# Second layer of a graph network: two weight slots swap roles each block, output weights split in the last head, three output tiles between the last weighted values

## The reference, cut to what matters

```python
cond = silu(emb @ f_w1 + f_b1) @ f_w2 + f_b2
for i in range(4):
    y = cond_layer_norm(x, cond, s1_w[i], s1_b[i], b1_w[i], b1_b[i])
    y = sparse_attention(y, src, dst, wq[i], bq[i], wk[i], bk[i], wv[i], bv[i], wo[i], bo[i])   # 4 heads of 128
    x = x + y
    y = cond_layer_norm(x, cond, s2_w[i], s2_b[i], b2_w[i], b2_b[i])
    x = x + relu(y @ m_w1[i] + m_b1[i]) @ m_w2[i] + m_b2[i]
```

## Time and profile before

| | us |
|---|---|
| runs, median of 3 (lowest, highest) | 2396.46 (2392.19, 2398.84) |
| the profiled execution, its own time | 2400.95 |
| span of its profile | 2399.2 |
| TensorE busy | 2106.9 (88%) |
| VectorE, ScalarE, GpSimd busy | 1584.8, 961.6, 643.8 |
| TensorE clock granted, mean | 0.948 of full speed |

### The profile page before, as it was taken

One profiled execution on the slowest core, in us unless ns is written; L12 is line 12 of the kernel. 1 busy time (PEld: TensorE's weight loads), 2 busy tenths in 40 slices (PEclk: granted clock), 3 DMA queues, 4 the chain that ended last, 5 costly groups with the idle time before them and its releaser, 6 DMA issues. The chain is left out here.

```text
span 2399.2 us, 38632 instructions
## 1 busy us (share of the span) xinstructions
PE 2106.9 (88%) x14446; PEld 1593.5 (66%) x14446; DVE 1584.8 (66%) x3086; ACT 961.6 (40%) x1418; POOL 643.8 (27%) x472
## 2 busy tenths in 40 slices
PE   6888979999899998899999899999898997878783
PEld 5885537788787887787788687788684544333331
DVE  8995344778564778554778554778655046898974
ACT  1112213666333666333666333666330031243442
POOL 0000015200543200544200544200420000476773
PEclk9999989999999999999999999999999997898997
DMA  1012301789511788511788611688946000000001
GB/s 59 34 45 46 104 23 61 130 149 159 118 57 37 136 141 151 128 41 52 117 146 155 138 38 56 114 148 147 201 103 145 16 20 2 0 0 0 1 1 43
DMA packets 488314, 195.74 MB, mean 82 GB/s; under 512 B 441241, under 2 KB 457625, under 8 KB 488133
## 3 DMA queue, kind: packets, MB, share of 16 engines
q1 hardware_dynamic: 488133, 193.31, 39.2%
HBM read 62.94 MB, written 25.45 MB: 37 GB/s over the span
## 5 line engine op out<-in xcount | busy, mean ns | idle before, releaser
L670 PE MATMUL psum<-turned_probability_parts,values_high 125*128 125x125 bf16 x1600 | 283.1, 223 | 55.0 <-DMA turned_probability_parts<-probability_parts 33.8
L859 DVE CUSTOM_DVE_ANT_0 probabilities<-psum,counts 125x1250 f32<-125x1250 f32 x160 | 233.6, 1460 | 125.7 <-PE psum L672 125.2
L1383 ACT ACTIVATE probabilities<-probabilities,row_peaks 125x1250 f32<-125x1250 f32 x160 | 214.5, 1341 | 177.4 <-DVE row_peaks L863 177.3
L672 PE MATMUL psum<-turned_probability_parts,values_low 125*128 125x125 bf16 x1600 | 282.4, 222 | 0.0
L671 PE MATMUL psum<-turned_probability_parts,values_high 125*128 125x125 bf16 x1600 | 282.2, 222 | 0.0
L1575 DVE SCALAR_TENSOR_TENSOR probability_parts<-probabilities,row_masses,probability_parts 125x1250 bf16<-125x1250 f32 x160 | 245.2, 1533 | 11.4 <-ACT probability_parts L1393 9.0
L1902 POOL TENSOR_TENSOR logs_and_shifts<-logs_by_source,target_shifts_spread 125x1250 f32<-125x1250 f32 x80 | 208.0, 2617 | 126.5 <-ACT target_shifts_spread L2035 67.0
L1393 ACT ACTIVATE probability_parts<-probabilities,row_masses 125x1250 bf16<-125x1250 f32 x160 | 214.0, 1338 | 41.8 <-DVE row_masses L871 34.3
L2141 PE MATMUL psum<-probabilities_turned,values_and_ones 125*65 125x512 f32 (+1 forms) x480 | 200.1, 563 | 22.1 <-ACT probabilities_turned L2052 11.8
L670 PEld LDWEIGHTS psum<-turned_probability_parts,values_high 125*128 125x128 bf16 x1600 | 159.6, 100 | 76.5 <-issue 73.5
L453 ACT ACTIVATE norm_std<-norm_moments,norm_eps 125x1 f32<-125x1 f32 x120 | 35.2, 294 | 345.6 <-DVE norm_moments L449 345.6
(11 more groups left out here) (291 smaller groups left out, 5048.4 us busy)
## 6 DMA issues: line engine op xcount, KB each, us to landing
weight_stage<-in_L_gnn_m_w SPq DMA_DIRECT2D x32, 256.0 KB, 2.7
block_inputs_kept<-nodes SPq DMA_DIRECT2D x8, 896.0 KB
counts_kept<-counts_by_target_rows SPq DMA_DIRECT2D x10, 625.0 KB, 3.6
logs_kept<-counts SPq DMA_DIRECT2D x1, 5468.8 KB
nodes<-block_inputs_kept SPq DMA_DIRECT2D x12, 448.0 KB
turned_probability_parts<-probability_parts SPq DMA_TRANSPOSE x320, 3.6
counts_by_target<-counts_kept SPq DMA_DIRECT2D x2, 2187.5 KB
logs_by_source<-logs_kept SPq DMA_DIRECT2D x1, 4375.0 KB
```

Source lines behind the costliest of these rows:

```text
L670: pe.matmul(out, lh, rh, start=first, stop=False, skip_group_check=True)
L672: return pe.matmul(out, ll, rh, start=False, stop=last, skip_group_check=True)
L859: dve.tensor_tensor_reduce(prob[0:TILE, T % 2, :], scores, fx.count_src[0:TILE, i, 0:NODES], scale, MASKED, ALU.add, ALU.max, p[:, 0:1]).t ...
L1383: nc.scalar.activation(prob[0:TILE, T % 2, :], prob[0:TILE, T % 2, :], ACT.Exp, bias=fx.peak[0:TILE, T % 2, 1:2], accum_out=fx.mass[0:TILE ...
```

## The change

The two slots are allocated with the same three layouts each. `scored_slot(b) = (b + 1) % 2` holds queries, keys and later m1; `attended_slot(b) = b % 2` holds wv, the attended rows and the first keys of the odd heads, later wo and then m2. So wo goes where the attended rows were (free once their low parts are made, at tile 3 of the last head; the fourth piece and the bias row wait for the last scores, as keys lie there), and m1 goes where queries and keys were. Slot A grows from 20000 to 20096 bytes, and everything above it moves up by 96.

- **Loads.** Pieces 14 and 15 of wo are issued by SP at tiles 6 and 7 of the last head (before: after T = 39), the bias row of wo at tile 8, ahead of the transposes of T = 39. m1's first two pieces and the bias row of m2 come right after the transposes of T = 39. The load of `nodes` waits for `pv_done` of T = 39.
- **Splits.** POOL does both parts of wo, in the last head. In `between` it does bias 0 to 3, two splits of m1, bias 4 and 5, the other two splits, bias 6 to 9.
- **Order of TensorE in the drain:** output rows 0, weighted 36, weighted 37, output rows 1 and modulation 0, weighted 38, output rows 2, turn 0 and modulation 1, weighted 39. DVE and ACT walk steps 0 to 2 between their own parts of T = 37, 38 and 39. The output rows of tiles 1 and 2 go to banks 4 and 5.

```diff
-SLOT_B_AT = SLOT_A_AT + PLANE
+SLOT_B_AT = SLOT_A_AT + 4 * 5024
...
+        def scored_slot(b):
+            return (b + 1) % 2
+        def attended_slot(b):
+            return b % 2
+        def output_bank(t):
+            return bank(3 + t) if t < 3 else bank(3 if t % 2 else 7)
...
         @block.sync
+                        if h == HEADS1 - 1 and i in (6, 7):
+                            weight(b, 14 + (i == 7), rows_of(wo, b, 2 + (i == 7)))
+                        if h == HEADS1 - 1 and i == 8:
+                            sp.wait_ge(qk_done, 40 * b + 40)
+                            bias_row(slot_row[attended_slot(b)], bo, b, 3 * b + 1)
...
-                sp.wait_ge(qk_done, 40 * b + 40)
-                bias_row(row_b, bo, b, 3 * b + 1)
-                for i in (2, 3):
-                    weight(b, 12 + i, rows_of(wo, b, i))
-                sp.wait_ge(o_done, 40 * b + 40)
+                for i in (0, 1):
+                    weight(b, 16 + i, rows_of(m1, b, i))
+                bias_row(slot_row[scored_slot(b)], b2, b, 3 * b + 2)
+                sp.wait_ge(pv_done, 40 * b + 40)
                 for k, t in enumerate(range(EARLY, TILES, 2)):
                     for a, z in ROW_PARTS:
                         sp.dma_start(fx.nodes[a:z, t:t + 2], kept[a:z, t:t + 2]).then_inc(x_back[k], 16)
-                for i in (0, 1):
-                    weight(b, 16 + i, rows_of(m1, b, i))
-                sp.wait_ge(att_low, 13 * b + 13)
-                bias_row(row_a, b2, b, 3 * b + 2)
...
         @block.gpsimd
-                    for t in range(6):
+                    for t in range(EARLY):
                         with_output_bias(t)
-                    pool.wait_ge(att_low, 13 * b + 13)
-                    for i in range(4):
-                        split(b, 16 + i, wa[0][:, i, :], wa[1][:, i, :])
+                    for i in range(2):
+                        split(b, 16 + i, first[0][:, i, :], first[1][:, i, :])
+                    for t in range(EARLY, 6):
+                        with_output_bias(t)
+                    for i in range(2, 4):
+                        split(b, 16 + i, first[0][:, i, :], first[1][:, i, :])
...
+                high, low = slot_weights[attended_slot(b)]
+                pool.wait_ge(att_low, 13 * b + HEADS1 - 1)
+                for i in range(12, 16):
+                    if i == 15:
+                        pool.wait_ge(qk_done, 40 * b + 40)
+                    split(b, i, high[:, i - 12, :], low[:, i - 12, :])
...
         @block.tensor
+                        if h == HEADS1 - 1 and i == TILES - 1:
+                            between_step(b, 0)
...
-                for i in range(TILES - LAG, TILES):
-                    weighted(HEADS1 - 1, i)
-                pe.wait_ge(scored, 40 * b + 40)
-                pe.wait_ge(o_done, 40 * b + 40)
+                weighted(HEADS1 - 1, TILES - 3)
+                pe.wait_ge(scored, 40 * b + 40)
+                between_step(b, 1)
+                weighted(HEADS1 - 1, TILES - 2)
+                between_step(b, 2)
+                weighted(HEADS1 - 1, TILES - 1)
...
         @block.scalar
-                def output_weights_high(i):
-                    act.wait_ge(qk_done, 40 * b + 40)
-                    act.wait_ge(stage_loaded[i % 2], 16 * (12 * b + i // 2 + 1))
-                    nc.scalar.activation(wb[0][:, i - 12, :], stage[:, i % 2, :], ACT.Copy).then_inc(split_high, 1)
...
+                attend(HEADS1 - 1, TILES - 3)
+                between_step(b, 0)
+                attend(HEADS1 - 1, TILES - 2)
+                between_step(b, 1)
+                between_step(b, 2)
+                attend(HEADS1 - 1, TILES - 1)
...
         @block.vector
-                        for i in range(TILES - LAG - 1, TILES):
-                            last_attended_low(i)
+                last_attended_low(TILES - 4)
+                for s in range(DRAIN):
+                    between_step(b, s)
+                    last_attended_low(TILES - 3 + s)
```

More of the change, by code:

```diff
@@ L809, in steps_of @@
         def steps_of(bp, more):
-            return range(0 if bp >= 0 else AFTER, AFTER + TILES + (more if bp < LAYERS1 - 1 else 0))
+            return range(DRAIN if bp >= 0 else AFTER, AFTER + TILES + (more if bp < LAYERS1 - 1 else 0))
         def kept_rows(t):
@@ L1034, in between @@
                 if b >= 0:
[L1035 to L1039, removed]
+                    first, second = slot_weights[scored_slot(b)], slot_weights[attended_slot(b)]
                     def with_output_bias(t):
@@ L1070, in between @@
                     for i in range(4):
-                        split(b, 20 + i, wb[0][:, i, :], wb[1][:, i, :])
+                        split(b, 20 + i, second[0][:, i, :], second[1][:, i, :])
                     for t in range(7, TILES):
@@ L1143, in turn_rows, with rows_product @@
                 mm.then_inc(y_turned, 1)
-            def rows_product(t, n, weights, split=None, attended=None):
+            def rows_product(t, out, weights, split=None, attended=None):
                 for c in range(CHUNKS):
@@ L1152, in rows_product @@
                         pe.wait_ge(att_low, attended + c + 1 + (t if c == CHUNKS - 1 else 0))
-                    mm = three(pe, bank(n)[0:TILE], [p[:, c, cols(t)] for p in pair_y], [p[:, c, :] for p in weights],
+                    mm = three(pe, out[0:TILE], [p[:, c, cols(t)] for p in pair_y], [p[:, c, :] for p in weights],
                                c == 0, c == CHUNKS - 1)
@@ L1216, in project, with between_step @@
                 mm.then_inc(proj_prod, 1)
+            def between_step(bp, s):
+                if bp >= 0 and s < TILES:
+                    output_rows(bp, s)
+                if bp >= 0 and s >= AFTER and s - AFTER < TILES:
+                    second_rows(bp, s - AFTER)
+                if norm_at(bp, s - 2):
+                    turn_rows(*norm_at(bp, s - 2))
+                if norm_at(bp, s - 1):
+                    modulation(*norm_at(bp, s - 1))
+                if bp >= 0:
+                    for k in HIDDEN_AT.get(s, ()):
+                        hidden_half(bp, k)
+                if bp < LAYERS1 - 1:
+                    if 0 <= s - AFTER - 4 < TILES:
+                        value_rows(bp + 1, s - AFTER - 4)
+                    for c in PROJECT_AT.get(s, ()):
+                        project(bp + 1, 0, c)
             def between(bp):
                 for s in steps_of(bp, 4):
[L1221 to L1236, removed]
+                    between_step(bp, s)
             for b in range(LAYERS1):
@@ L1414, in _ @@
                             projected_high(b, *projection_at(h, i))
+                        if not more and i == TILES - 1:
+                            high_part(h, i)
                         if i >= LAG:
@@ L1505, in hidden_low, with between_step @@
                                   ALU.subtract).then_inc(h_low, 1)
+            def between_step(bp, s):
+                if norm_at(bp, s - 2):
+                    finish(*norm_at(bp, s - 2))
+                if bp >= 0 and s < TILES:
+                    dve.wait_ge(o_prod, 10 * bp + s + 1)
+                    dve.wait_ge(x_biased, 10 * bp + s + 1)
+                    if s < EARLY:
+                        dve.wait_ge(part_low, 40 * bp + 40)
+                    dve.tensor_tensor(fx.nodes[0:TILE, s, :], output_bank(s)[0:TILE], kept_rows(s),
+                                      ALU.add).then_inc(residual, 1)
+                    dve.wait_ge(residual, 10 * bp + s + 1)
+                if bp == LAYERS1 - 1 and s > AFTER:
+                    joined_normed(s - AFTER - 1)
+                if bp >= 0 and s >= AFTER and s - AFTER < TILES:
+                    t = s - AFTER
+                    dve.wait_ge(m_prod, 10 * bp + t + 1)
+                    dve.wait_ge(x2_biased, 10 * bp + t + 1)
+                    dve.tensor_tensor(fx.nodes[0:TILE, t, :], bank(4 * (t % 2) + 3)[0:TILE], fx.nodes[0:TILE, t, :],
+                                      ALU.add).then_inc(x_done, 1)
+                    dve.wait_ge(x_done, 10 * bp + 10 + t + 1)
+                    if bp == LAYERS1 - 1:
+                        joined(t)
+                if norm_at(bp, s):
+                    stats(*norm_at(bp, s))
+                if norm_at(bp, s - 1):
+                    scale(*norm_at(bp, s - 1))
+                if norm_at(bp, s - 3):
+                    turned_low(*norm_at(bp, s - 3))
+                if bp >= 0:
+                    for k in HIDDEN_AT.get(s - 1, ()):
+                        if k % 2 == 1:
+                            hidden_low(bp, k // 2)
+                if bp < LAYERS1 - 1:
+                    for c in PROJECT_AT.get(s - 1, ()):
+                        projected_low(bp + 1, 0, c)
```

184 lines of the change are left out of this document (76 added, 108 removed).

## The result

The changed kernel takes 2433.2 us (median of 4, 2430.52 to 2435.03) against 2396.58 before: ratio 1.0143, 95% interval 1.0118 to 1.0167 (the two medians alone divide to 1.0153, inside it). It is 37 us slower, where 4 us faster was forecast, and outside the range of 2379 to 2403.

The account below looks back on a forecast made before the run. TensorE, busy 88%, bounds it; only its idle time (about 9 us a block) and low clock can give. Block gains 2.8, 2.8, 1.6, -2.8 sum to 4.4, less 0.4: 4 us faster, 2392.5 us median, range 2379 to 2403.

Parts of the forecast that it names:

- What it removes and adds: Drain: wo's copies and subtractions leave it, POOL splits wo in the last head; output rows 0 leave TensorE about S + 3.1.
- S: End of a block's last scores on TensorE, zero point of the drain's times; 605.41 us in block 0 before the change.
- Point 1: Drain on TensorE: weighted 36, before at S + 1.16, starts at 3.1 behind output rows 0 and ends at 4.9.
- points 2 to 5: Drain, after S: T = 38's high transpose 5.0, bias row 12.2, residual 0 13.5, norm 0 ends 19.6, then weighted 39.
- E: Time after S when weighted 39 ends (`pv_done`): taken as 23.9 us, between 22.4 and 24.4.
- What is late next: Before the first hidden half: two m1 pieces load behind `nodes`, so TensorE waits about 2 us in blocks 0 to 2.
- E + 13.7: First hidden half's start in blocks 0 to 2: 9.5 us for loads, 4.0 for two splits, 0.2 more.
- E + 18.5: First hidden half's start in block 3, where 1.27 MB of counts load between `nodes` and piece 18; block 3 gain -2.8 us.
- the walk keeps its order, so a gain or loss at that point stays: Walk after the first hidden half: order unchanged, so no further gain or loss was counted there.
- the address or a worse queue in the last head: Slower rival: transposes last longer from the address moved 96 bytes, or last head's queue worsens; up to 2416; chance 0.15.
- Drain as short as its parts: Well-faster rival: clock stays up, m1 pieces in time; 17 us gained, 2379.5, at the limit 2360; chance 0.27.
- signs listed as right: Output rows 0 directly after scores; T = 38 transpose 2 us later; idle before turn 0 and hidden half; weighted 39 S + 20 to 22.

Follow-up runs that it names:

- e2: Changed kernel with pieces 14 and 15 of wo loaded at tiles 4 and 5 of the last head, not 6 and 7: 2407.3 us, 1.0039 of before.
- e3: Changed kernel with output rows 0 behind weighted 37 on TensorE, not ahead of weighted 36; loads stay late: 2391.7 us, 0.9975 of before.
- e6: Changed kernel with wo pieces 14 and 15 at tiles 4 and 5 and wo's bias row at tile 7, not 8: 2379.2 us, 0.9920 of before.
- e7: Changed kernel with wo pieces and bias row early, output rows 0 behind weighted 37, weighted 39 ahead of turn 0: 2384.2 us, 0.9943 of before.
- e8: e7 with all four m1 pieces issued ahead of nodes, and POOL's last two splits ahead of bias 4 and 5: 2371.5 us, 0.9879 of before.
- e9: e6, keeping the changed kernel's order, with m1's first two pieces at tile 8, last two ahead of nodes, POOL as in e8: 2359.6 us, 0.9843 of before.
- e4: Changed kernel with weighted 39 ahead of turn 0 and modulation 1 in step 2: 2409.5 us, 1.0053 of before.
- e5: Changed kernel with the drain's old order back on all three engines; slots, loads and splits as changed: 2392.9 us, 0.9971 of before.
- e1: Kernel before with only slot A grown from 20000 to 20096 bytes, moving all above by 96: 2396.4 us, 0.9999 of before.

## Why the prediction was wrong

**The step that failed** is in "What it removes and adds": a split is 1.98 us, "three are done before S, the fourth starts at S". That was the length of the work without the arrival of its data. Measured, the third split starts 2.1, 0.1, 0.1 and 1.9 us after S in blocks 0 to 3 and the fourth 5.8, 4.4, 4.6 and 5.0 after, since their pieces are issued behind the transposes of T = 36 and 37. The trace of before held the answer. There SP sent those transposes at

```profile
600.29 1.33 SPq L942 DMA_TRANSPOSE turned_probability_parts<-probability_parts  x1
601.66 1.68 SPq L944 DMA_TRANSPOSE turned_probability_parts<-probability_parts  x1
603.72 2.01 SPq L942 DMA_TRANSPOSE turned_probability_parts<-probability_parts  x1
605.78 1.60 SPq L944 DMA_TRANSPOSE turned_probability_parts<-probability_parts  x1
```

so a load behind T = 36 can leave at 603.34 = S - 2.1 and one behind T = 37 at 607.38 = S + 2.0 (block 0), and the bias row, 256 KB as well, took 4.2 us to land. The last three matmuls of output rows 0, put at S + 2.4, start at S + 8.9, 6.5, 6.6 and 7.0 in blocks 0 to 3.

**What it pulled with it.** Point 1 (weighted 36 at 3.1) was measured as 10.3, 7.9, 8.1 and 8.5; with the pieces in time, 3.0 to 3.1 (e2). From there points 2 to 5 hold with their numbers: in e2 residual 0 starts at 13.1 to 13.9 (13.5), turn 0 at 19.3 to 20.0 (19.6), and E, put at 23.9, is 23.6 to 24.6; in the changed kernel it is 29.8 to 32.8. e3 shows the same from the other side, by taking the waiting product out of the way. Of the 37 us e2 gives back 26; that is the price of this step.

**What is late next.** "E + 13.7" for the hidden half in blocks 0 to 2 was right: 32.7 + 13.7 = 46.4 against 46.0 measured in the changed kernel, and 13.3 to 14.3 in e2, e6 and e7. So was "E + 18.5" in block 3 (19.0 in the changed kernel, 18.9 in e2). e8 takes that wait away by the order of the loads.

**A second step failed behind the windows.** e2 has the pieces in time and is still 9 us slower than the kernel before. The prediction put the walk behind the windows at nothing ("the walk keeps its order, so a gain or loss at that point stays"). The order did stay, the clock did not. The 40 us behind block 3's window, before the change and in the changed kernel after its wait of 7.34 us:

```profile
1732.15:1772.15 40.00, 38.41 (x273) 35.36 (x272) 24.61 (x42) 13.86 (x29) 24.94 (x21) 1.00 0.82 185
1755.77:1795.77 40.00, 38.40 (x252) 35.31 (x253) 20.83 (x36) 12.25 (x25) 24.86 (x22) 0.94 0.72 176
```

TensorE is as busy, but does 252 matmuls in place of 273. From the first to the last matmul of the hidden halves the walk of block 3 takes 59.5 us in place of 57.2, and those of blocks 1 and 2, behind waits of 1.4 and 1.8 us, 57.8 and 57.9 in place of 56.3. Block 0's, behind a wait of 1.5 us, takes 54.8 in place of 56.1, at a granted clock of 1.00: a short wait isn't always followed by the lower level. In block 3 the runs with a wait of 6.2 to 7.6 us (e2, e3, e6, e7 and the changed kernel) all take 59.5 to 60.1; of those without one, four take 57.1 to 57.2 and e9 58.4; e4, with 2.8 us, takes 58.3.

A further 4.4 us lie in the third and fourth layers, whose code is the same: 582.3 us from the third layer's first product to the end, against 577.8. The profiles fall into two groups there: the changed kernel, e2, e5 and e8 with 582.3 to 582.9, all others with 577.8 to 578.7. e5 and e8 have no wait ahead of block 3's hidden half, and e3, e6 and e7 have long ones, so these 4.4 us don't come from that wait. What does make the groups stays open.

**The rivals.** A slower result had a chance of 0.15 for the address or a worse queue in the last head. The address is refuted by e1, and the attention parts of the changed kernel are no longer than before in blocks 0 to 2 (187.1 to 189.5 us against 188.3 to 189.6; block 3 187.1 against 185.9). The forecast's sign was wrong by a mechanism that I had listed nowhere: the prediction asked what waits behind norm 0 on TensorE, and didn't ask what waits behind output rows 0. "Drain as short as its parts" named the conditions of a real gain rightly (clock up, m1's pieces in time), and e9 with 2359.6 comes out at what it called the limit, 2360. That the two numbers meet is luck in part: e9 also moves the loads of wo, its bias row and m1, and gains by the higher clock what it still loses in idle time. Of the signs listed as right, the idle time ahead of turn 0 (4.66 us, by DVE's norm) and the wait before the hidden half, longest in block 3, came; "output rows 0 directly after the last scores" came too, in half. The high transpose of T = 38 "about 2 us later" did not: it went out 8 to 10 us later, and weighted 39 started at 26.4 to 29.4 and not at 20 to 22.

## What to carry to other kernels

Work put into an engine's idle time must have its operands there before the work that it is put ahead of; otherwise the engine waits in order, and the items behind it (here two weighted tiles, and through them a transpose, a bias row, a norm and a load) inherit the wait. A load's place in a loop is the time at which the issuing queue gets there, not that tile's time on another engine: read it from the queue's own timeline. In the new order, two loads issued two tiles sooner gave 26 us, one load a tile sooner 28, and m1 ahead of nodes 13 more. No run has these early loads with the old order, so what the reordering itself is worth is not measured; only that slots, order and loads together give 1.6%, and slots alone 0.3%.

## What was not expected of the hardware

POOL's subtraction of a 128 x 512 piece took 2.35 to 2.36 us at 604.12 and 607.80, where it ran beside DVE's `low_part` (`SCALAR_TENSOR_TENSOR`, median 1.52 us), against 1.29 alone. The eleven traces hold 73 such meetings of 0.2 us or more, and the order of the two starts tells them apart. In 21 of them DVE began first, by 0.08 us or more, and POOL's subtraction took 2.08 to 2.56 us. In the other 52 POOL's began first (in one, 0.03 us behind DVE's recorded start) and took 1.26 to 1.31; DVE's operation took up to 2.6 us instead, the longer the more the two overlapped. So the later one pays. Such a delay is about 1 us; in the waits for the splits of wo the late landing of the pieces is the larger part.

The 96 bytes made no difference that 10 runs could tell.
